# The first half's residual moved from VectorE to ScalarE and an accumulating DMA, in a two-layer convolution kernel on one core

## The chip, the core and the metric

The kernel runs on one core of a Trainium2 chip. The metric is the device time of one execution in microseconds (us). The engines work on queues of their own and meet through semaphores: PE (TensorE, matmuls), DVE (VectorE), ACT (ScalarE), POOL (GpSimd) and SP (SyncE, which here only issues DMAs). Lines such as L847 are lines of the kernel.

## What is computed

The input is 16 images of 128 channels by 64 x 64 pixels. Two layers follow one another, each with a group normalisation (`_gn`) ahead and a residual.

```python
def _L0_conv_ref(x, g_pos, g_neg, bias, input_factor, output_factor):
    v = dac(x * input_factor)
    ...
    patches = unfold2d(v, KH, KW, SH, SW)
    fv = patches + CUBIC * patches ** 3
    g = g_pos - g_neg
    outs = [jnp.einsum('bctfyx,ocyx->btfo', fv, g[i]) for i in range(WP - 1)]
    mem_out = adc(outs[-1])
    for i, bit in enumerate(reversed(range(WP - 1))):
        mem_out = mem_out + adc(outs[i]) * 2.0 ** bit
    mem_out = mem_out * output_factor
    result = mem_out + bias
...
x = x + _L0_conv_ref(_gn(x), ...)
x = x + _L1_conv_ref(_gn(x), Wq, Wk, Wv, B, Wm)
```

The first layer is a 3 x 3 convolution with three sets of weights ("planes"); each plane's sum is rounded and clipped, the three are added with weights, scaled, given a bias and added to x. The second layer projects each pixel to 64-channel queries, keys and values, forms exponential sums, takes a ratio, projects back to 128 channels and adds.

## The kernel before, in words

An image is held in SBUF as one of four buffers `xr`, used in turn, 128 channels by 4096 pixels in f32, and is worked on in four quarters of 1024 pixels (`PX`) or two halves of 2048 (`HPX`). The images run through a software pipeline: in phase p the kernel makes the first layer's convolution of image p, the second layer of image p-1, and the statistics and input rows of image p+1. A phase has 36 slots, `SLOTS = 6 * STEPS`, and each engine has a loop over these slots of its own. Which work stands at which slot is written out by hand in the tables at the head of the file (`X1_STATS`, `BIAS`, `RESIDUAL`, `DOUBLE`, `HIGH`, `Z_ACT` and so on), and within a slot the order of the lines in `phase` decides. A slot number over 35 means a slot of the next phase. An engine works its queue in order, so an instruction that waits holds all that stands behind it.

A phase has six steps n of six slots: two halves h of three planes i. For a step, PE makes six products of the convolution: two into bank B (`low_pair`, at place 0 and 1), two into a bank of A (place 2 and 3), and the last two into that same bank of A one step later (`outer`, place 4 and 5). The banks of A alternate, `A[n % 2]`. At each product two matmuls with the high parts and one with the low parts run for each of three rows of taps (L504 to L506). ScalarE copies bank B to SBUF (`copy_m2`, L839, place 2 of the step), VectorE mixes it with bank A (`mix_middle`, L1195 to L1207), and when the last products are in, ScalarE rounds the bank to int16 (`adc_round`, L847) into the plane's buffer `u[i]`. PE may use a bank of A again when the rounding of two steps earlier is done, which it waits for ahead of its first product into the bank:

```python
if j == 1 and (prev or n >= 2):
    pe.wait_ge(rounded, nth(p, STEPS, n - 2))
```

For step 0 of an image that is the rounding of step 4 of the image before, which stands at slot 0 of ScalarE's queue. Ahead of it, at slot 35, ScalarE doubles plane 0 of the second half (`double`, L855), for which VectorE waits in `combine_planes` (L1213 to L1218, slot 0).

When a half's planes are there, VectorE clips the last, adds it (L1225, L1228) and makes the residual (L1231, slot 23 for the first half, slot 8 of the next phase for the second), `xr = u[1] * fin + xr`. ScalarE has added the bias to `xr` before (`add_bias`, L859, slots 17 and 32). The statistics for the second normalisation are taken by ScalarE from the finished `xr`, two passes for each quarter with accumulation (`channel_stats`, L803 to L812). The quarters of the first half stand at slots 26 and 31, those of the second half at slots 8 and 9 of the next phase, and VectorE reads all four at slot 12.

The second layer of image p-1 runs in quarters: ScalarE makes z (`z_split`, L875 and L880, slots 18, 25, 35, 41), POOL its low part (`z_rest`, L1499), PE the projections (L586, behind the wait for L839), ScalarE the exponentials (L884, L896), VectorE their product with the values (`weighted_values`, L1283), PE the sums (L617), ScalarE the logarithm (L890, L892), VectorE the ratio (L1292 to L1300), PE the projection back (L639), ScalarE the eviction (L904) and POOL an accumulating DMA of 512 KB into `xr` (`add_mix`, L1532). The first layer's input rows are made by ScalarE (L749, L759, L769), VectorE (L1107 to L1151) and POOL (`rows_low`, L1525). SP issues the loads of image p+2 and the stores of finished quarters.

The buffer `shared` holds weights in the making at the start and small pieces afterwards. In the last phases there is no next image, and the second layer of the last two images has slots of its own (`TAIL`).

Of the kernel before, what the change touches and what calls it, by code (L numbers as in the profile page):

```python
# [34 lines left out]
PX = ROWS * W  # L35
# [34 lines left out]
BIAS = (17, 32)  # L70
X1_STATS = (26, 31, 8, 9)
# [31 lines left out]
def conv_layers_kernel(nc, x, g_pos, g_neg, bias, in_factor, out_factor, Wq, Wk, Wv, Bm, Wm, out):  # L103
# [6 lines left out]
    with ctx:  # L110
# [3 lines left out]
        def sem(name):  # L114
            return ctx.enter_context(nc.semaphore(name))
# [10 lines left out]
        shared = sb("shared", [P, NP * 4 * 3 * P + 4 * 3 * P])  # L126
        y2 = [shared[:, k * PX:(k + 1) * PX] for k in range(2)]
# [145 lines left out]
        biased = sem("biased")  # L273
        first_done = sem("first_done")
# [448 lines left out]
        def _(act):  # L723
# [96 lines left out]
            def stats_x1(image, m, q, before):  # L820
                act.wait_ge(first_done, nth(image, HALVES, q // 2))
                channel_stats(1, xr[m], image, q, before)
# [18 lines left out]
            def adc_round(p, n, first):  # L841
                h, i = divmod(n, NP)
                act.wait_ge(conv_ready, nth(p, STEPS, n))
                if not first or h:

                    act.wait_ge(first_done if i else summed, nth(p, HALVES, h - 1))
                nc.scalar.copy(u[i].rearrange("p (t k c) -> p k t c", k=4, c=W)[:, 0:4:3],  # L847
                               A[n % 2][:, :, :].rearrange("p e (t w) -> p e t w", w=W)).then_inc(rounded, 1)
# [8 lines left out]
            def add_bias(p, m, h):  # L857
                xh = xr[m][:, h * HPX:(h + 1) * HPX]
                nc.scalar.activation(xh, xh, ACT.Identity, bias=bcol[:, :]).then_inc(biased, 1)  # L859
# [64 lines left out]
            def phase(p, m, images):  # L924
# [3 lines left out]
                for slot in range(SLOTS):  # L928
# [32 lines left out]
                    if cur and slot in BIAS:  # L961
                        add_bias(p, m, BIAS.index(slot))
# [40 lines left out]
        def _(dve):  # L1003
# [161 lines left out]
            def mix_middle(p, n, images):  # L1165
# [25 lines left out]
                if i == 1 and (prev or h):  # L1191
                    dve.wait_ge(first_done, nth(p, HALVES, h - 1))
# [27 lines left out]
            def first_residual(p, m, h):  # L1220

                xh = xr[m][:, h * HPX:(h + 1) * HPX]
                dve.wait_ge(rounded, nth(p, STEPS, NP * h + 2))
                dve.wait_ge(inner_made, nth(p, STEPS, NP * h + 2))
                nc.vector.tensor_scalar(u[2], u[2], CLIP, -CLIP, ALU.min, ALU.max).then_inc(clipped_last, 1)  # L1225
                dve.wait_ge(summed, nth(p, HALVES, h))
                dve.wait_ge(clipped_last, nth(p, HALVES, h))
                nc.vector.tensor_tensor(u[1], u[1], u[2], ALU.add).then_inc(combined, 1)  # L1228
                dve.wait_ge(combined, nth(p, HALVES, h))
                dve.wait_ge(biased, nth(p, HALVES, h))  # L1230
                nc.vector.scalar_tensor_tensor(out=xh, in0=u[1], scalar=fin[:, :], in1=xh, op0=ALU.mult, op1=ALU.add  # L1231
                                               ).then_inc(first_done, 1)

            def last_residual(m):
# [6 lines left out]
                dve.wait_ge(biased, nth(p, HALVES, h))  # L1241
# [18 lines left out]
            def last_sums(m):  # L1260
# [3 lines left out]
                dve.wait_ge(first_done, HALVES * B)  # L1264
# [84 lines left out]
            def phase(p, m, images):  # L1349
# [3 lines left out]
                for slot in range(SLOTS):  # L1353
# [19 lines left out]
                    if prev and cur and slot == RESIDUAL[1]:  # L1373
                        first_residual(p - 1, before, 1)
# [13 lines left out]
                    if cur and slot == RESIDUAL[0]:  # L1388
                        first_residual(p, m, 0)
# [48 lines left out]
        def _(pool):  # L1438
# [95 lines left out]

            def second_layer(p, m, slot, images):
# [8 lines left out]
            def phase(p, m, images):  # L1544
                prev2, prev, cur, nxt = images
                before, two_before = (m + 3) % RING, (m + 2) % RING
                for slot in range(SLOTS):
                    second_layer(p, m, slot, images)
                    if cur and slot in LOW[2:]:
                        rows_low(p, m % 2, LOW.index(slot))  # L1550
                    if nxt and slot in LOW[:2]:
                        rows_low(p + 1, 1 - m % 2, LOW.index(slot))
# [41 lines left out]
```

## Time and profile before

| | |
|---|---|
| median of 3 runs | 1522.66 us (1522.54 to 1523.33) |
| profiled execution, its own time | 1522.15 us |
| its span, first to last instruction | 1520.4 us |
| mean granted TensorE clock | 0.983 |
| busy: PE, VectorE, ScalarE, POOL | 1430.8, 1400.2, 1193.8, 528.1 us |
| residual L1231 on VectorE | 31 instructions, 85.8 us |
| bias L859 on ScalarE | 32 instructions, 63.9 us |
| accumulating DMAs of 512 KB on POOL | 60 |

The profile shows one execution. Busy time is the time in which an engine had an instruction at work; waits for semaphores and the issuing of DMAs are not in it. A line of the timeline gives the start in us from the span's start, the duration, the engine, the line, the operation, output and input by the program's names, and in brackets the idle time of the engine just before, with what ended it. The granted clock is TensorE's: 1.00 is its upper level of 2.4 GHz and 0.50 its lower level of 1.2 GHz. Consecutive matmuls overlap, so a matmul's duration is longer than the distance between two starts.

### The profile page before, as it was taken

What the parts mean: (1) busy time and instruction counts of PE and PEld (TensorE: products, weight loads), DVE (VectorE), ACT (ScalarE), POOL (GpSimd) and SP (SyncE); (2) the same over time, 40 slices, a digit from 0 to 9 for tenths busy, and PEclk for the clock granted to TensorE, in tenths of its full rate; (3) what the DMA queues carried; (4) which work ended last, traced back from release to release, by engine and by line L of the source; (5) the groups of instructions that cost most, each with busy time, mean ns of one, the idle gap of its engine ahead of it and who ended that gap; (6) DMA issues with size and microseconds to landing.
All of it is one profiled execution on the core that took longest, in us unless ns stands there. A gap on an engine that the chain in (4) does not pass through costs nothing.

```text
span 1520.4 us, 24553 instructions
## 1 busy us (share of the span) xinstructions
PE 1430.8 (94%) x8560; PEld 659.2 (43%) x8560; DVE 1400.2 (92%) x2185; ACT 1193.8 (79%) x1561; POOL 528.1 (35%) x503
## 2 busy tenths in 40 slices
PE   2799999999999999999999999999999999999975
PEld 2444444444444444444444444444444444444432
DVE  6879999999999999999999999999999999999766
ACT  4547788788978878897887889788797978876563
POOL 3111334333433433343343334434333443433312
PEclk9799999999999999999999999999999999999997
DMA  5011011223123222312322231232223123212232
GB/s 209 1 56 42 15 29 46 94 56 111 35 56 105 57 84 56 111 39 56 101 56 84 56 112 37 53 108 56 84 56 112 32 56 108 57 28 57 56 84 84
DMA packets 29181, 103.92 MB, mean 68 GB/s; under 512 B 4032, under 2 KB 4224, under 8 KB 29056
## 3 DMA queue, kind: packets, MB, share of 16 engines
q1 hardware_dynamic: 20416, 70.86, 12.6%
q0 software_dynamic: 8640, 31.46, 10.9%
q8 instruction: 71, 1.16, 0.3%
q14 instruction: 54, 0.44, 0.1%
HBM read 37.29 MB, written 33.55 MB: 47 GB/s over the span
## 4 chain that ended last, share of the span: by engine, by line
DVE 51%; PE 25%; issue 16%; ACT 5%; DVEq 1%; POOL 1%; DMA 0%; SPq 0%; ACTq 0%; POOLq 0%
PE A L504 5%; PE A L506 4%; PE A L505 4%; DVE duo L1135 4%; DVE A L1198 3%; DVE A L1207 3%; DVE uall L1201 3%; DVE uall L1228 3%; DVE duo L1195 3%; DVE uall L1203 3%; DVE A L1199 3%; DVE duo L1196 3%; DVE f L1112 2%; PE B L504 2%; DVE t L1147 2%
## 5 line engine op out<-in xcount | busy, mean ns | idle before, releaser
L504 PE MATMUL A<-T,WH 128*128 128x504 f16 (+1 forms) x1152 | 438.5, 381 | 0.0
L505 PE MATMUL A<-T,WH 128*128 128x504 f16 (+1 forms) x1152 | 437.5, 380 | 0.0
L506 PE MATMUL A<-T,WL 128*128 128x504 f16 (+1 forms) x1152 | 437.5, 380 | 0.0
L1525 POOL TENSOR_TENSOR T<-t,T 128x512 f16<-128x512 f32 x189 | 259.5, 1399 | 421.8 <-ACT T L769 421.8
L1499 POOL TENSOR_TENSOR zl<-z,zh 128x512 f16<-128x512 f32 x120 | 160.5, 1354 | 404.9 <-ACT zh L880 404.9
L812 ACT ACTIVATE junk<-xr,shift 128x1024 f16<-128x1024 f32 x244 | 280.1, 1148 | 5.4
L504 PE MATMUL B<-T,WH 128*128 128x504 f16 (+1 forms) x576 | 222.0, 385 | 19.9 <-DVE T L1161 11.5
L505 PE MATMUL B<-T,WH 128*128 128x504 f16 (+1 forms) x576 | 221.9, 385 | 0.0
L506 PE MATMUL B<-T,WL 128*128 128x504 f16 (+1 forms) x576 | 221.8, 385 | 0.0
L504 PEld LDWEIGHTS A<-T,WH 128*128 128x128 f16 x1152 | 115.4, 100 | 165.5 <-issue 47.6
L506 PEld LDWEIGHTS A<-T,WL 128*128 128x128 f16 x1152 | 112.7, 98 | 136.2
L505 PEld LDWEIGHTS A<-T,WH 128*128 128x128 f16 x1152 | 112.8, 98 | 118.0
L749 ACT ACTIVATE q<-xr,bi,sc 128x1024 int16<-128x1024 f32 x64 | 79.2, 1240 | 68.5 <-DVE f L1112 46.5
L839 ACT COPY m<-B 128x1024 f32<-128x1024 f32 x96 | 95.9, 999 | 36.9 <-PE B L506 36.9
L769 ACT CAST T<-t 128x512 f16<-128x512 f32 x192 | 105.9, 614 | 21.8 <-DVE t L1151 21.7
L847 ACT CAST uall<-A 128x1024 int16<-128x1024 f32 x96 | 96.1, 1002 | 33.3 <-PE A L506 33.1
L504 PEld LDWEIGHTS B<-T,WH 128*128 128x128 f16 x576 | 57.0, 99 | 91.6 <-ACT T L769 11.6
L1532 POOL DMA_DIRECT2D xr<-shared x60 | 53.8, 897 | 108.2 <-ACT shared L904 108.2
L884 ACT ACTIVATE shared<-L 128x512 f32<-128x512 f32 x61 | 36.1, 592 | 70.3 <-PE L L586 70.3
L506 PEld LDWEIGHTS B<-T,WL 128*128 128x128 f16 x576 | 57.1, 99 | 70.2 <-issue 3.6
L505 PEld LDWEIGHTS B<-T,WH 128*128 128x128 f16 x576 | 57.0, 99 | 69.3 <-issue 3.3
L1231 DVE SCALAR_TENSOR_TENSOR xr<-uall,fin,xr 128x2048 f32<-128x2048 int16 x31 | 85.8, 2768 | 1.1
(186 smaller groups left out, 2573.0 us busy)
## 6 DMA issues: line engine op xcount, KB each, us to landing
xr<-in_x_dram SPq DMA_DIRECT2D x64, 512.0 KB, 5.7
out_dram<-xr SPq DMA_DIRECT2D x64, 512.0 KB, 2.7
xr<-shared POOLq DMA_DIRECT2D x60, 512.0 KB, 4.5
xr<-in_L_conv_g_pos_dram SPq DMA_DIRECT2D x3, 576.0 KB, 9.9
xr<-in_L_conv_g_neg_dram SPq DMA_DIRECT2D x3, 576.0 KB, 10.9
xr<-in_L_conv_Wm_dram SPq DMA_DIRECT2D x2, 32.0 KB, 9.0
xr<-in_L_conv_Wq_dram SPq DMA_DIRECT2D x1, 32.0 KB, 11.7
xr<-in_L_conv_Wk_dram SPq DMA_DIRECT2D x1, 32.0 KB, 11.6
```

What stands on the lines that cost most here:

```text
L504: nc.tensor.matmul(to, wh, th, start=fresh and y == 1, stop=False, skip_group_check=True)
L505: nc.tensor.matmul(to, wh, tl, start=False, stop=False, skip_group_check=True)
L506: done = nc.tensor.matmul(to, wl, th, start=False, stop=y == 2, skip_group_check=True)
L749: nc.scalar.activation(q16[b][:, :], xr[m][:, q * PX:(q + 1) * PX], ACT.Identity, bias=bi1[:, :], scale=sc1[:, :]).then_inc(leveled, 1)
L769: nc.scalar.copy(T[:, 0, pair, g * TILES:(g + 1) * TILES, :, :], t32[:, pair]).then_inc(th_ready, 1)
L812: nc.scalar.activation(junk[:, :], src[:, q * PX:(q + 1) * PX], func, bias=shift[which][:, :], accum_out=moments[which][:, k, q:q + 1]).th ...
L839: nc.scalar.copy(m2[:, :, :], low_pair[:, :, :]).then_inc(m2_copied, 1)
L847: nc.scalar.copy(u[i].rearrange("p (t k c) -> p k t c", k=4, c=W)[:, 0:4:3], A[n % 2][:, :, :].rearrange("p e (t w) -> p e t w", w=W)).the ...
L1135: nc.vector.tensor_tensor(flat, f[:, at + 2:at + 2 + ROWS, :], f[:, at:at + ROWS, :], ALU.subtract).then_inc(delta_made, 1)
L1231: nc.vector.scalar_tensor_tensor(out=xh, in0=u[1], scalar=fin[:, :], in1=xh, op0=ALU.mult, op1=ALU.add).then_inc(first_done, 1)
L1499: nc.gpsimd.tensor_tensor(zl[0][:, cols], z32[:, cols], zh[0][:, cols], ALU.subtract).then_inc(zl_ready, 1)
L1525: last = nc.gpsimd.tensor_tensor(low, t32[:, pair, :, :, :].rearrange("p t e w -> p (t e w)"), high, ALU.subtract)
```

## The change

For the first half of each image the bias pass of ScalarE at slot 17 and the residual of VectorE at slot 23 go. VectorE still clips and adds the last plane (now `sum_planes`). ScalarE then writes `y1 = u[1] * fin + bcol` into a free part of `shared` (`first_output`, slot 25), and POOL adds it to `xr` with an accumulating DMA of 1 MB (`first_add`, slot 26). The two statistics passes over the first half wait for that DMA and move from slots 26 and 31 to slots 34 and 35. The waits that protect `u[1]` and `u[2]` are named anew: plane 4's mixing on VectorE waits for `first_output`, and the roundings into `u[1]` and `u[2]` wait for `first_output` and for the sum. The second half is made as before. The change's title also speaks of PE's second layer sorted by shape; the diff has no line of PE.

```diff
-BIAS = (17, 32)
-X1_STATS = (26, 31, 8, 9)
+OUTPUT = 25
+OUTPUT_ADD = 26
+BIAS = 32
+X1_STATS = (34, 35, 8, 9)
...
+        y1 = shared[:, 2 * PX:4 * PX]
...
             def stats_x1(image, m, q, before):
-                act.wait_ge(first_done, nth(image, HALVES, q // 2))
+                if q < 2:
+                    act.wait_ge(first_added, nth(image, 16, 15))
+                else:
+                    act.wait_ge(first_done, nth(image, 1, 0))
...
-                    act.wait_ge(first_done if i else summed, nth(p, HALVES, h - 1))
+                    if i == 0:
+                        act.wait_ge(summed, nth(p, HALVES, h - 1))
+                    elif i == 2:
+                        act.wait_ge(combined, nth(p, HALVES, h - 1))
+                    elif h:
+                        act.wait_ge(y1_made, nth(p, 1, 0))
+                    else:
+                        act.wait_ge(first_done, nth(p, 1, 0, 1))
...
-            def add_bias(p, m, h):
-                xh = xr[m][:, h * HPX:(h + 1) * HPX]
+            def first_output(p):
+
+
+                act.wait_ge(combined, nth(p, HALVES, 0))
+                if isinstance(p, int) and p == 0:
+                    act.wait_ge(small_done, 1)
+                    act.wait_ge(w_turned, 9)
+                else:
+                    act.wait_ge(first_added, nth(p, 16, 15, 1))
+                nc.scalar.activation(y1, u[1], ACT.Identity, bias=bcol[:, :], scale=fin[:, :]).then_inc(y1_made, 1)
+
+            def add_bias(p, m):
+                xh = xr[m][:, HPX:2 * HPX]
                 nc.scalar.activation(xh, xh, ACT.Identity, bias=bcol[:, :]).then_inc(biased, 1)
...
-                if i == 1 and (prev or h):
-                    dve.wait_ge(first_done, nth(p, HALVES, h - 1))
+                if i == 1 and h:
+                    dve.wait_ge(y1_made, nth(p, 1, 0))
+                elif i == 1 and prev:
+                    dve.wait_ge(first_done, nth(p, 1, 0, 1))
...
+            def first_add(p, m):
+
+
+                waits_apart(pool, (y1_made, nth(p, 1, 0)))
+                nc.gpsimd.dma_start(xr[m][:, 0:HPX], y1, accum_op=ALU.add).then_inc(first_added, 16)
```

## Rows read from the trace of the kernel before

**Rows 1.** The page, busy us (share of the span) and number of instructions.

```profile
PE 1430.8 (94%) x8560; PEld 659.2 (43%) x8560; DVE 1400.2 (92%) x2185; ACT 1193.8 (79%) x1561; POOL 528.1 (35%) x503
```

**Rows 2.** Stretches of an image: us, busy us of each engine, PEclk, DMA.

```profile
706.90:795.35 88.45, 86.93 (x528) 39.57 (x527) 85.02 (x133) 74.49 (x99) 33.19 (x31) 1.00 0.26 72
...
sum 707.60, PE 695.89 PEld 317.76 DVE 676.60 ACT 596.35 POOL 263.94; mean PE 86.99 PEld 39.72 DVE 84.58 ACT 74.54 POOL 32.99
```

**Rows 3.** Waits: engine, line, waited for, us in total, times, longest.

```profile
PE L L586 <- ACT m L839: 10.0, 15, 1.1
...
PE L L617 <- DVE shared L1283: 9.1, 15, 0.7
...
ACT q L749 <- POOL bi L1483: 22.0, 16, 2.7
```

**Rows 4.** Timeline of ScalarE, 726 to 755 us.

```profile
726.83 1.00 ACT L839 COPY m<-B 128x1024 f32<-128x1024 f32 x1
...
735.15 1.15 ACT L812 ACTIVATE junk<-xr,shift 128x1024 f16<-128x1024 f32 x1
...
737.57 0.99 ACT L839 COPY m<-B 128x1024 f32<-128x1024 f32 x1
...
740.14 0.60 ACT L884 ACTIVATE shared<-L 128x512 f32<-128x512 f32 x1 [1.58 <-PE L L586]
...
743.73 1.66 ACT L769 CAST T<-t 128x512 f16<-128x512 f32 x3 [0.45 <-DVE t L1151]
...
749.57 1.91 ACT L855 ACTIVATE uall<-uall 128x2048 int16<-128x2048 int16 x1
...
751.38 0.99 ACT L847 CAST uall<-A 128x1024 int16<-128x1024 f32 x1
...
752.27 0.20 ACT L803 ACTIVATE shift<-xr 128x1 f32<-128x1 f32 x1
...
754.93 0.99 ACT L839 COPY m<-B 128x1024 f32<-128x1024 f32 x1
```

**Rows 5.** Timeline of PE, 731 to 754 us.

```profile
731.71 0.38 PE L504 MATMUL B<-T,WH 128*128 128x512 f16 x1
...
738.61 1.05 PE L586 MATMUL L<-zh,wqkv 128*64 128x512 f16 x8 [0.90 <-ACT m L839]
...
744.44 1.09 PE L617 MATMUL L<-shared,eb 64*64 64x256 f32 x16 [0.62 <-DVE shared L1283]
...
753.25 0.38 PE L504 MATMUL A<-T,WH 128*128 128x512 f16 x1
```

**Rows 6.** Timeline of VectorE, 724 to 754 us.

```profile
724.46 2.35 DVE L1231 SCALAR_TENSOR_TENSOR xr<-uall,fin,xr 128x2048 f32<-128x2048 int16 x1
...
734.53 0.68 DVE L1195 TENSOR_TENSOR duo<-A,m 128x512 f32<-128x512 f32 x1
...
753.17 0.68 DVE L1213 TENSOR_SCALAR uall<-uall 128x2048 int16<-128x2048 int16 x1
```

**Rows 7.** PE's timeline at 137.50, and the stretch from 137.34.

```profile
137.50 0.59 PE L504 MATMUL B<-T,WH 128*128 128x512 f16 x1 [2.30 <-issue]
...
137.34:140.75 3.41, 3.25 (x8) 1.17 (x9) 3.34 (x7) 2.66 (x6) 0.06 (x1) 0.50 0.00 0
```

**Rows 8.** The last images: timeline of ScalarE and PE, and the stretch from 1465.13.

```profile
1462.05 1.23 ACT L875 ACTIVATE z<-xr,bi,rs 128x1024 f32<-128x1024 f32 x1
...
1465.09 0.64 PE L586 MATMUL L<-zh,wqkv 128*64 128x512 f16 x2 [2.28 <-DVE shared L1300]
...
1465.13:1468.54 3.41, 3.41 (x18) 1.32 (x18) 0.00 (x0) 2.53 (x3) 2.45 (x3) 0.50 0.14 28
```

**Rows 9.** ScalarE's L875 by shape; L1532's DMAs to landing; POOL's timeline.

```profile
L875 ACT ACTIVATE z<-xr,bi,rs 128x1024 f32<-128x1024 f32 x60 | 73.8, 1230 | 0.0
...
DMA to landing us min/median/max: 4.5/4.5/6.0
...
734.34 3.52 POOL L1525 TENSOR_TENSOR T<-t,T 128x512 f16<-128x512 f32 x3 [5.00 <-ACT T L769]
```

More of the change, by code:

```diff
@@ L273, in conv_layers_kernel @@
         biased = sem("biased")
+        y1_made = sem("y1_made")
+        first_added = sem("first_added")
         first_done = sem("first_done")
@@ L960, in phase @@
                         double(p, DOUBLE.index(slot))
-                    if cur and slot in BIAS:
-                        add_bias(p, m, BIAS.index(slot))
+                    if cur and slot == OUTPUT:
+                        first_output(p)
+                    if cur and slot == BIAS:
+                        add_bias(p, m)
                     if cur and slot in HIGH[2:]:
@@ L1218, in combine_planes, with sum_planes @@
                 nc.vector.tensor_tensor(u[1], u[0], u[1], ALU.add).then_inc(summed, 1)
-            def first_residual(p, m, h):
-                xh = xr[m][:, h * HPX:(h + 1) * HPX]
+            def sum_planes(p, h):
                 dve.wait_ge(rounded, nth(p, STEPS, NP * h + 2))
@@ L1228, in first_residual @@
                 nc.vector.tensor_tensor(u[1], u[1], u[2], ALU.add).then_inc(combined, 1)
-                dve.wait_ge(combined, nth(p, HALVES, h))
-                dve.wait_ge(biased, nth(p, HALVES, h))
+            def first_residual(p, m):
+                xh = xr[m][:, HPX:2 * HPX]
+                dve.wait_ge(combined, nth(p, HALVES, 1))
+                dve.wait_ge(biased, nth(p, 1, 0))
                 nc.vector.scalar_tensor_tensor(out=xh, in0=u[1], scalar=fin[:, :], in1=xh, op0=ALU.mult, op1=ALU.add
@@ L1240, in last_residual @@
                 dve.wait_ge(summed, nth(p, HALVES, h))
-                dve.wait_ge(biased, nth(p, HALVES, h))
+                dve.wait_ge(biased, nth(p, 1, 0))
                 for c in range(2):
@@ L1263, in last_sums @@
                 count = 1.0 * PX
-                dve.wait_ge(first_done, HALVES * B)
+                dve.wait_ge(first_done, B)
                 for h in range(2):
@@ L1373, in phase @@
                     if prev and cur and slot == RESIDUAL[1]:
-                        first_residual(p - 1, before, 1)
+                        sum_planes(p - 1, 1)
+                        first_residual(p - 1, before)
                     if not cur and slot == 3:
@@ L1388, in phase @@
                     if cur and slot == RESIDUAL[0]:
-                        first_residual(p, m, 0)
+                        sum_planes(p, 0)
                     if nxt and slot in QUANTISE:
@@ L1550, in phase @@
                         rows_low(p, m % 2, LOW.index(slot))
+                    if cur and slot == OUTPUT_ADD:
+                        first_add(p, m)
                     if nxt and slot in LOW[:2]:
```

## The prediction

> **What bounds the kernel now.** I read the page's busy line first: PE is busy 94% of the span and VectorE 92%, so either could be the bound [rows 1]. The page's chain runs mostly through VectorE, but a chain cannot tell who has slack, so I went to stretches of one image each: eight of them last 707.60 us, 88.45 us an image, and in the mean PE is busy 86.99 of these, VectorE 84.58, ScalarE 74.54 [rows 2]. The waits of PE settle it. In the steady part it waits at two places only, once an image each: for ScalarE's copy L839 (10.0 us in 15 waits, 0.67 us each) and for VectorE's L1283 (9.1 us in 15, 0.61 us each) [rows 3]. So PE is the bound, and all that the change can gain there is 10.0 + 9.1 = 19.1 us, however much VectorE work it removes.
>
> What PE waits for without showing it has to be read from the order of the work. The first matmuls into bank A of an image (slot 2) wait, at L550, for ScalarE's rounding of plane 4 of the image before (L847 at slot 0). ScalarE ends that rounding at 751.38 + 0.99 = 752.37 [rows 4]; PE starts the matmuls at 753.25 [rows 5]. The slack is 0.88 us. This is the number on which the forecast turns.
>
> **The change, part by part.** The diff touches nothing on PE: the sorting of the second layer in the title has no line in it, and I cost it at nothing.
>
> *VectorE* loses the L1231 of each image's first half, 16 instructions of 2.35 us (one of these at 724.46 [rows 6]). VectorE then comes to plane 4 (734.53) and to L1283 about 2.3 us earlier, which ends PE's wait for L1283. It waits anew for ScalarE's output pass before plane 4: that pass ends near 729.2 (below), and VectorE gets there at 734.53 - 2.35 = 732.2, so the wait costs nothing; if the pass came over 3 us later, VectorE would wait and give back part of the 2.35 us.
>
> *ScalarE, slot 17 to slot 25.* The bias pass of the first half goes. Behind it ScalarE waits for POOL's scale anyway (22.0 us in 16 waits [rows 3]), so no gain. The new pass reads 2048 int16 and writes f32 with a bias and a scale. The nearest rows are L855, of equal width and int16 input (1.91 us at 749.57 [rows 4]), and L875, with both factors, 1.23 us for half the width, so 2.46 us [rows 9]. I take 2.3 us. VectorE's sum is done at 724.46, and ScalarE comes to the pass at 726.83, where the copy of plane 4 (L839) now starts [rows 4, 6]. That copy moves to 729.1 and ends at 730.1; PE needs it at 731.71 [rows 5]. Cover 1.6 us, cost nothing at either bound.
>
> *POOL and the DMA.* One accumulating issue of 1 MB an image is added. POOL waits for the output pass in its queue; the next instruction behind it starts at 734.34 after an idle 5.00 us, so nobody behind it is held [rows 9]. The 512 KB form lands 4.5 us after issue, at most 6.0 [rows 9]. For 1 MB I bound it by 4.5 and 2 x 6.0 = 12 us and take 9: issued near 729.3, landed near 738.3, at the worst 741.3. The statistics that wait for it start near 745 (below). Cost nothing. SP's queue is not touched, and its loads are needed only at slot 0.
>
> *ScalarE, slots 26 and 31 to slots 34 and 35.* Here is the price. Two statistics passes cost 754.93 - 752.27 = 2.66 us (with the shift) and 737.57 - 735.15 = 2.42 us [rows 4], 5.08 us together. At slot 31 the pass stood ahead of the copy L839 for which PE waited; taking it away ends that wait. But it does not leave ScalarE earlier at the end of the image: behind the copy, ScalarE waits for PE (1.58 us before 740.14) and is paced by it [rows 4]. From 740.14 to the rounding at 751.38 ScalarE has one wait, 0.45 us before 743.73; the rest is work back to back, and both statistics now stand inside this stretch, ahead of the doubling and of the rounding.
>
> The sum for this image: ScalarE enters the stretch 0.90 us earlier (PE's wait for the copy, gone), saves the 0.45 us (VectorE's T is earlier), and does 5.08 us more. The rounding ends at 752.37 - 0.90 - 0.45 + 5.08 = 756.10. PE, freed of 0.90 and 0.62 us [rows 5], is ready at 753.25 - 1.52 = 751.73. It stands idle for 4.4 us and goes on at 756.10, 2.85 us later than before. With the mean wait of 0.67 us in place of 0.90 it is 3.08; I take 3.0 us an image. VectorE's gain is not passed on either: its next step waits for the doubling, which ends near 755.1, while it began that step at 753.17 [rows 6].
>
> *What an idle PE costs beyond the wait.* After an idle stretch of 2.30 us PE started at 137.50, and the 3.41 us from 137.34 ran at a granted 0.50, the 1.2 GHz level; near the end, 2.28 us of idle were followed by 3.41 us at 0.50 as well [rows 7, 8]. Work at half speed for 3.41 us costs 1.7 us. The two short waits of an image leave the clock at its full level, 1.00 [rows 2]. The new wait is 4.4 us, longer than either that were followed by the low level, so I add 1.7 us an image. The Trainium skill, "TensorE: Matmul & The Clock Gate" (section on HAM oscillation), warns that waits between bursts of matmuls throw the array back to the low clock and that every round of a loop then pays for it. The trace shows this for single gaps; none of its steady images does. By that rule alone the sum would be the one with the clock term, without it the rival below.
>
> *How often, and the ends.* The two short waits come at 15 places; the full pattern (second layer between slots 21 and 35, next image at slot 2) is there 14 times, from image 1 to image 14. Behind image 0 there is no second layer and ScalarE has waits enough: I count 0. At the tail, z of image 14's last part (1462.05) moves behind one statistics pass, 2.66 us, and PE's start at 1465.09 waits for it [rows 8]; some 2.5 us go to the end.
>
> Sum: 14 x (3.0 + 1.7) + 2.5 = 68.3 us. The profiled execution took 1522.15 us, 0.51 under the median of the three runs, 1522.66. The forecast for the median is 1522.66 + 68.3 = 1591, rounded to **1590 us**. A measurement of this kernel tells about 0.2% (3 us) from no change.
>
> **The rivals.**
>
> *The clock holds.* If the 4.4 us fall so that the low level lies mostly inside the idle stretch, only 14 x 3.0 + 2.5 = 44.5 us are left: **1567 us**. For it: the steady part shows 1.00 throughout; against it: both idle stretches above were shorter. 0.20.
>
> *Faster: PE's two waits go and no new one comes.* Place: the release of bank A at slot 2. Price: the 19.1 us of waits go, **1503 us**. It decides if ScalarE's rounding comes no later than PE's readiness, that is if its stretch from 740.14 takes 4.4 us less than my sum, for instance because the waits that the trace puts on PE there are not what paces ScalarE. For it: VectorE has less to do and all that it feeds comes earlier. Against: the rows of the stretch stand back to back. 0.07.
>
> *Worse than the forecast.* The low clock lasts for two stretches of 3.41 us: 14 x 1.7 = 24 us more, **1614 us**. Or the DMA lands over 16 us after its issue, and each us beyond costs 14 us. For it: 1 MB in one accumulate is nowhere in this trace, and loads of 512 KB run beside it. Against: none of the smaller ones took over 6.0 us. 0.09.
>
> *The parts cancel* (a shorter ScalarE stretch, no low clock): within 3 us of before, **1523 us**. 0.04.
>
> **How the numbers follow.** Forecast 0.60, then 0.20, 0.07, 0.09 and 0.04. Faster holds 0.07, same 0.04, slower 0.60 + 0.20 + 0.09 = 0.89. The range takes in the forecast, the clock rival and the longer low clock, with the per-image term between 2.0 and 3.1 us: 14 x 2.0 + 2.5 = 30.5, so from 1553 to 1614 us.
>
> **What would show it.** Right: in the waits of PE a new entry once an image, bank A waiting for ScalarE's L847 copy, near 4.4 us; the entries for L839 and L1283 gone; the granted clock dips once an image, and PE's share falls below 94%; VectorE's 16 passes gone from its busy time, its idle time larger, ended by the doubling. Wrong: no wait of PE at slot 2, or a wait of ScalarE for the new DMA ahead of the statistics at slot 34, or VectorE waiting for the output pass ahead of plane 4. A steady image under 88.45 us would overturn the whole argument.

## The result, and the profile after

The change makes the kernel slower: 1607.99 us (median of 4 runs, 1606.51 to 1608.83) against 1522.64 us before on the same chip, a ratio of 1.0559 with an interval of 1.054 to 1.0577. That is 85.4 us more where 68.3 were forecast. The sign, the place and the kind of the loss came as predicted; the size was 17 us short.

The page's busy line after, to be read against [rows 1]:

```profile
PE 1459.3 (91%) x8560; PEld 663.8 (41%) x8560; DVE 1391.4 (87%) x2169; ACT 1195.3 (74%) x1561; POOL 555.7 (35%) x519
```

VectorE has 16 instructions less, but only 8.8 us of busy time less, where 16 x 2.35 = 37.6 us were taken away. PE does the same 8560 matmuls and is busy 28.5 us longer, which fits matmuls at a lower clock (below).

The waits after, as engine, line, what it waits for, us in total, times, longest:

```profile
PE A L509 <- ACT uall L862: 57.4, 15, 4.1
...
PE L L622 <- DVE shared L1316: 11.6, 14, 0.9
...
PE L L591 <- ACT m L847: 3.6, 4, 3.1
```

The first row is new. Bank A now waits for ScalarE's rounding (L862, which was L847) in every image: 1.17 us behind image 0, then 4.05 us in 13 images and 3.52 in one. This is the slack of 0.88 us of [rows 4, 5] turned into a wait. The third is what is left of the wait for ScalarE's copy, 10.0 us in [rows 3]: 3.1 of these 3.6 us fall in the last image. But the second, VectorE's L1316 (L1283 before), did not go: it was 9.1 us and is 11.6.

ScalarE's timeline in a middle image, through the stretch that answers to 740 to 755 us of [rows 4] (start, us, engine, line, what, idle before and releaser):

```profile
683.04 2.01 ACT L885 ACTIVATE xr<-xr,bcol 128x2048 f32<-128x2048 f32 x1
685.65 1.66 ACT L774 CAST T<-t 128x512 f16<-128x512 f32 x3 [0.59 <-DVE t L1179]
...
689.50 1.15 ACT L817 ACTIVATE junk<-xr,shift 128x1024 f16<-128x1024 f32 x1
...
694.13 1.14 ACT L817 ACTIVATE junk<-xr,shift 128x1024 f16<-128x1024 f32 x1
...
696.55 1.89 ACT L870 ACTIVATE uall<-uall 128x2048 int16<-128x2048 int16 x1
698.35 0.99 ACT L862 CAST uall<-A 128x1024 int16<-128x1024 f32 x1
```

Each quarter has two passes; the first of each is shown. PE's timeline in the same image:

```profile
686.36 1.09 PE L622 MATMUL L<-shared,eb 64*64 64x256 f32 x16 [0.76 <-DVE shared L1316]
...
699.39 0.61 PE L509 MATMUL A<-T,WH 128*128 128x512 f16 x1 [4.05 <-ACT uall L862]
```

Both statistics stand ahead of the doubling and the rounding, as the diff says, and PE goes on with bank A 0.05 us after the rounding has ended.

These rows and those of before can be cut into two parts, from one such rounding to the next (a middle image in each kernel, not the same one). The rounding of the image before ended at 604.57 + 0.99 = 605.56:

```profile
604.57 0.99 ACT L862 CAST uall<-A 128x1024 int16<-128x1024 f32 x1
```

In the kernel before it ended at 663.61:

```profile
662.62 0.99 ACT L847 CAST uall<-A 128x1024 int16<-128x1024 f32 x1
```

From there to PE's sums (L617 before, L622 after) it was 744.44 - 663.61 = 80.83 us [rows 5], and is 686.36 - 605.56 = 80.80. From the sums to the end of the next rounding it was 752.37 - 744.44 = 7.93 us [rows 4, 5], and is 699.34 - 686.36 = 12.98. So the whole difference between these images, 5.02 us, lies in the second part, and it is the two statistics passes, 5.08 us in [rows 4]. The first part, in which VectorE lost 2.35 us of work, is not a tenth of a us shorter. The other middle images say the same: the second part is 13.0 us in all 13 images with both parts, against 7.9 to 8.2, and the first 80.5 to 81.0 in eight and 81.5 to 82.4 in five, against 80.4 to 80.9 (once 81.7).

Where those 2.35 us went stands in VectorE's and POOL's timelines:

```profile
665.57 1.23 DVE L1257 TENSOR_TENSOR uall<-uall 128x2048 int16<-128x2048 int16 x1
...
669.70 2.18 DVE L1163 TENSOR_TENSOR duo<-f 128x1024 f32<-128x1024 f32 x1
671.80 1.64 DVE L1166 SCALAR_TENSOR_TENSOR duo<-f 128x512 f32<-128x512 f32 x1
...
681.84 1.23 DVE L1163 TENSOR_TENSOR duo<-f 128x1024 f32<-128x1024 f32 x1
```

```profile
669.45 3.45 POOL L1533 TENSOR_TENSOR zl<-z,zh 128x512 f16<-128x512 f32 x2 [6.96 <-ACT zh L906]
```

Beside POOL's subtraction the same two instructions that take 1.23 and 0.69 us at 681.84 and 682.99 in this image took 2.18 and 1.64, together 1.90 us more; and POOL's pair took 3.45 us. In the kernel before, VectorE had reached only its work on PSUM (four instructions from 726.73) when that subtraction ran, and came to the transform behind it. The rows there, POOL's subtraction first, then VectorE's sum, its work on PSUM and the transform:

```profile
727.07 2.27 POOL L1499 TENSOR_TENSOR zl<-z,zh 128x512 f16<-128x512 f32 x2 [7.18 <-ACT zh L880]
```

```profile
723.20 1.22 DVE L1228 TENSOR_TENSOR uall<-uall 128x2048 int16<-128x2048 int16 x1
...
726.73 0.69 DVE L1292 TENSOR_TENSOR L<-L,shared 128x512 f32<-128x512 f32 x1
...
729.71 1.22 DVE L1135 TENSOR_TENSOR duo<-f 128x1024 f32<-128x1024 f32 x1
```

With the residual gone, VectorE is through with the work on PSUM sooner, and the transform slides beside the subtraction. VectorE also starts the sum ahead of all this later: 60.01 us behind the rounding, against 723.20 - 663.61 = 59.59 before. The 0.42 us and the 1.90 us make up the 2.35 but for 0.03.

The clock after, as stretches (us, busy us of PE, PEld, VectorE, ScalarE and POOL, granted clock, DMA share, GB/s):

```profile
605.20:608.61 3.41, 2.99 (x8) 1.05 (x9) 3.17 (x5) 3.26 (x7) 0.00 (x0) 0.50 0.65 148
697.40:704.23 6.83, 4.84 (x12) 1.78 (x13) 5.52 (x8) 6.73 (x11) 0.03 (x1) 0.50 0.59 154
```

Each of the 14 images has one such stretch at 0.50 (1.2 GHz), which begins between 2.0 us ahead of PE's start at bank A and 1.3 us behind it; nine last 3.41 us and five 6.83. From that start of PE to the next one it is 94.5 to 95.4 us behind the five longer ones, and 93.5 to 94.0 behind eight of the shorter (the ninth leads into the last image). Against the same images of before that is 6.5 us more in the mean for the five and 5.0 for the eight, so a longer stretch costs 1.5 us on top, 7.4 us for all five.

At the end there is one wait more, in ScalarE's timeline of the last image and in PE's:

```profile
1515.60 2.09 ACT L881 ACTIVATE shared<-uall,bcol,fin 128x2048 f32<-128x2048 int16 x1 [3.06 <-DVE uall L1257]
1517.60 0.99 ACT L847 COPY m<-B 128x1024 f32<-128x1024 f32 x1
```

```profile
1518.64 1.05 PE L591 MATMUL L<-zh,wqkv 128*64 128x512 f16 x8 [3.08 <-ACT m L847]
```

The output pass waits for VectorE's sum, the copy of bank B stands behind it in ScalarE's queue, and PE waits for the copy.

The two new pieces of work cost what the prediction took for them. ScalarE's output pass takes 2.09 us (2.3 taken), and the DMA answers to [rows 9] so (issues, KB each, median us from issue to landing):

```profile
xr<-shared POOLq DMA_DIRECT2D x60, 512.0 KB, 4.6
xr<-shared POOLq DMA_DIRECT2D x16, 1024.0 KB, 8.1
```

### The profile page after: what moved, and what is told of

Same layout as the page of the kernel before. It is cut to its first block, busy times and chain, and to the rows that moved or that the text cites. A ratio compares the mean times of both kernels' runs of the same rounds, so it can differ in the third digit from the quotient of the medians.

```text
span 1606.5 us, 24563 instructions
## 1 busy us (share of the span) xinstructions
PE 1459.3 (91%) x8560; PEld 663.8 (41%) x8560; DVE 1391.4 (87%) x2169; ACT 1195.3 (74%) x1561; POOL 555.7 (35%) x519
## 4 chain that ended last, share of the span: by engine, by line
DVE 46%; issue 19%; PE 18%; ACT 14%; POOL 1%; DMA 1%; DVEq 1%; SPq 0%; ACTq 0%; POOLq 0%
DVE duo L1163 4%; PE A L509 4%; PE A L510 3%; PE A L511 3%; ACT junk L817 3%; DVE A L1228 3%; DVE duo L1166 3%; DVE A L1237 3%; DVE uall L1231 3%; DVE duo L1225 2%; DVE duo L1226 2%; DVE A L1229 2%; DVE uall L1233 2%; ACT z L901 2%; DVE f L1140 2%
## 5 line engine op out<-in xcount | busy, mean ns | idle before, releaser
L509 PE MATMUL A<-T,WH 128*128 128x504 f16 (+1 forms) x1152 | 450.4, 391 | 57.4 <-ACT uall L862 57.4
L510 PE MATMUL A<-T,WH 128*128 128x504 f16 (+1 forms) x1152 | 448.3, 389 | 0.0
L511 PE MATMUL A<-T,WL 128*128 128x504 f16 (+1 forms) x1152 | 447.3, 388 | 0.0
L1533 POOL TENSOR_TENSOR zl<-z,zh 128x512 f16<-128x512 f32 x120 | 176.5, 1488 | 492.1 <-ACT zh L906 492.1
L509 PEld LDWEIGHTS A<-T,WH 128*128 128x128 f16 x1152 | 117.6, 102 | 235.7 <-ACT uall L862 64.8
L510 PEld LDWEIGHTS A<-T,WH 128*128 128x128 f16 x1152 | 115.1, 100 | 122.3 <-issue 10.7
L847 ACT COPY m<-B 128x1024 f32<-128x1024 f32 x96 | 96.1, 1001 | 60.5 <-PE B L511 32.8
L862 ACT CAST uall<-A 128x1024 int16<-128x1024 f32 x96 | 96.1, 1001 | 43.0 <-PE A L511 43.0
L1163 DVE TENSOR_TENSOR duo<-f 128x1024 f32<-128x1024 f32 x64 | 91.7, 1432 | 7.8 <-POOL T L1559 4.0
L509 PEld LDWEIGHTS B<-T,WH 128*128 128x128 f16 x576 | 56.9, 99 | 91.3 <-ACT T L774 11.6
L1316 DVE SCALAR_TENSOR_TENSOR shared<-L,shared 128x512 f32<-128x512 f32 x61 | 41.8, 686 | 60.4 <-ACT shared L910 59.6
```

The costliest lines, as they stand in the source:

```text
L509: nc.tensor.matmul(to, wh, th, start=fresh and y == 1, stop=False, skip_group_check=True)
L510: nc.tensor.matmul(to, wh, tl, start=False, stop=False, skip_group_check=True)
L511: done = nc.tensor.matmul(to, wl, th, start=False, stop=y == 2, skip_group_check=True)
L847: nc.scalar.copy(m2[:, :, :], low_pair[:, :, :]).then_inc(m2_copied, 1)
L1163: nc.vector.tensor_tensor(flat, f[:, at + 2:at + 2 + ROWS, :], f[:, at:at + ROWS, :], ALU.subtract).then_inc(delta_made, 1)
L1533: nc.gpsimd.tensor_tensor(zl[0][:, cols], z32[:, cols], zh[0][:, cols], ALU.subtract).then_inc(zl_ready, 1)
```

## The experiments

The main theory is that the place of the two statistics passes, ahead of the doubling and the rounding, costs nearly everything, by PE's wait for bank A and by the low clock behind it. The rivals were the new DMA traffic and VectorE's slower instructions.

**The statistics alone.** The kernel before with nothing but the two slots changed:

```diff
-X1_STATS = (26, 31, 8, 9)
+X1_STATS = (34, 35, 8, 9)
```

> The kernel before, with the statistics of the first half moved from slots 26 and 31 to 34 and 35 and nothing else: no new pass, no new DMA, the residual stays on VectorE. Order theory (the two passes stand ahead of ScalarE's rounding of plane 4, for which PE waits before bank A): PE waits 5.08 - 0.88 - 0.67 = 3.5 us an image at bank A and has one dip of the clock worth 1.7 us, 14 times, and 2.5 us at the tail: about 1522.6 + 75 = 1598 us, at least 1575. Traffic theory (the loss comes from the new pass and from the accumulating DMA of 1 MB, which slow the engines beside them): at most 1545 us, and no wait at bank A over 2 us.

It took 1621.49 us, ratio 1.0646 (1.0618 to 1.0674). Its waits:

```profile
PE A L504 <- ACT uall L847: 57.4, 15, 4.1
...
PE L L617 <- DVE shared L1283: 12.8, 14, 0.9
...
PE L L586 <- ACT m L839: 6.2, 15, 0.6
```

The bank's wait is the same to a tenth as with the whole change, without the DMA and with the residual still on VectorE. The two slots alone cost 99 us, 23 us more than the number expected, and more than the change; the rest of the change gives back about 13. Part of that is the clock: in this run 13 of the 14 images have a stretch of 6.83 us at 0.50, against five in the changed kernel. The traffic rival is out, and so is the thought that the move of the residual itself is what hurts.

**Nearly no statistics.** The changed kernel, the first two quarters' passes over 8 columns:

```diff
-nc.scalar.activation(junk[:, :], src[:, q * PX:(q + 1) * PX], func, bias=shift[which][:, :],
+cols = 8 if which and q < 2 else PX
+nc.scalar.activation(junk[:, 0:cols], src[:, q * PX:q * PX + cols], func, bias=shift[which][:, :],
```

> The changed kernel, with the statistics of the first half taken over 8 columns of each quarter in place of 1024 (the rest of the first half's statistics is left out); every instruction, wait and DMA stays. The four passes shrink from 1.15 us to about 0.2 us. Order theory: the wait of PE at bank A goes, the clock stays at 1.00 through the middle images, and what is left is the wait for VectorE's L1316 (0.8 us an image) and the wait in the last image: 1510 to 1527 us. Traffic theory: the pass and the DMA are still there, so the time stays over 1580 us.

It took 1531.48 us, ratio 1.0059 (1.004 to 1.0078), 4 us over the upper end of what was expected. Of PE's waits these are left:

```profile
PE L L622 <- DVE shared L1317: 11.7, 14, 0.9
...
PE A L509 <- ACT uall L863: 9.6, 14, 1.0
```

None of the 14 images has a stretch at 0.50 any more. 76 of the 85 us hang on the length of these passes. The wait at L622 is still there, so it does not come from the statistics, and without them nothing is gained over the kernel before, though VectorE has a pass less to do.

**One quarter nearly free**, to see whether the wait goes with the length of the work:

```diff
-cols = 8 if which and q < 2 else PX
+cols = 8 if which and q == 1 else PX
```

> The changed kernel, with the statistics of the second quarter alone (slot 35) taken over 8 columns in place of 1024; the rest of that quarter's statistics is left out. Order theory: ScalarE's stretch is 2 x 0.85 = 1.7 us shorter, so PE's wait at bank A falls from 4.2 to about 2.5 us an image, 14 x 1.7 = 24 us. The clock tells the rest: idle stretches of 2.3 us were followed by 0.50 in the kernel before, so I expect the dips to stay in most images, 1584 us; if the clock needs longer idle stretches than this one, the dips go and it is 24 us less, 1560 us. Rival (the time goes with the number of passes on ScalarE, not with where PE waits): 14 x 1.7 us at most and the wait at bank A unchanged.

It took 1576.92 us, ratio 1.037 (1.0353 to 1.0388), between the two numbers expected. The wait at bank A is 33.6 us in 14 images, 2.4 each, halfway between 0.7 with hardly any passes and 4.05 with both: it goes with the length of the work ahead of the rounding. The low clock was still there in 12 of the 14 images, for 3.41 us each.

**VectorE's work put back.** The changed kernel with a pass of 1536 columns on VectorE where the residual stood (its result is overwritten before use):

```diff
+dve.wait_ge(combined, nth(p, HALVES, 0))
+dve.wait_ge(mid_mixed, nth(p, STEPS, 3))
+nc.vector.scalar_tensor_tensor(out=duo_flat, in0=u[1][:, 0:PX + HALF], scalar=fin[:, :],
+                               in1=duo_flat, op0=ALU.mult, op1=ALU.add).then_inc(idle_made, 1)
+dve.wait_ge(idle_made, nth(p, 1, 0))
```

> The changed kernel, with a pass of the same kind as the removed residual put back on VectorE at slot 23 (1536 wide where the residual was 2048 wide, about 1.9 us, into scratch that is written anew before it is read). Order theory: VectorE waits 3.3 us an image for the doubling, so the work is hidden: 1600 to 1620 us. If VectorE's freed time had been worth its length, 16 x 1.9 = 30 us come on top: about 1638 us.

It took 1617.94 us, ratio 1.0629 (1.0609 to 1.0649): 10 us more than the change, 0.6 us for each of the 16 passes, which take 1.82 us each. Some of it is again the clock: eight images have the stretch of 6.83 us, against five. VectorE's groups by shape, in this kernel:

```profile
L1164 DVE TENSOR_TENSOR duo<-f 128x1024 f32<-128x1024 f32 x64 | 78.1, 1220 | 5.8 <-POOL T L1565 1.8
...
L1167 DVE SCALAR_TENSOR_TENSOR duo<-f 128x512 f32<-128x512 f32 x64 | 43.7, 683 | 0.0
```

and in the changed kernel:

```profile
L1163 DVE TENSOR_TENSOR duo<-f 128x1024 f32<-128x1024 f32 x64 | 91.7, 1432 | 7.8 <-POOL T L1559 4.0
...
L1166 DVE SCALAR_TENSOR_TENSOR duo<-f 128x512 f32<-128x512 f32 x64 | 57.2, 893 | 0.0
```

With work in that place the two instructions are back at their old durations; without it they take 13.6 + 13.5 = 27.1 us more over the run, of the 37.6 us that the change took off VectorE.

**The last image's output pass later**, behind the copy for which PE waits:

```diff
-if cur and slot == OUTPUT:
+if cur and slot == (OUTPUT if nxt else 27):
...
-if cur and slot == OUTPUT_ADD:
+if cur and slot == (OUTPUT_ADD if nxt else 27):
```

> The changed kernel, with the output pass and its DMA of the last image alone at slot 27, behind ScalarE's copy for plane 4 and the exponential of slot 26. If the wait of PE at 1518.64 in the last image (3.5 us between two matmuls, and 3.41 us at the low clock behind it) comes from the output pass standing ahead of that copy, it goes: 3.2 + 1.7 = 4.9 us less, about 1603 us. If it comes from something else in the tail: 1608 us as before.

It took 1602.93 us, ratio 1.0528 (1.0505 to 1.0551): 5 us less, as expected. The wait of 3.1 us is gone from PE's waits, and with it the stretch at 0.50 behind it; the next one, some 30 us later, lasts 6.83 us in place of 3.41.

**The bias pass away from the stretch.** In the changed kernel L885 stands at 683.04, ahead of the cast for T:

```diff
-BIAS = 32
+BIAS = 17
```

> The changed kernel, with the second half's bias pass (2.0 us) at slot 17 in place of 32, so out of ScalarE's stretch ahead of the rounding. If ScalarE's stretch alone paces bank A, the wait falls from 4.2 to 2.2 us: 14 x 2.0 = 28 us, about 1580 us or 20 us less where dips of the clock go with it. If VectorE's T at slot 29, which ScalarE waits for 0.6 us ahead of L774 even now, paces the stretch, ScalarE waits 2.0 us longer there and nothing is gained: 1600 to 1610 us.

It took 1609.15 us, ratio 1.0575 (1.0559 to 1.0592): nothing gained by taking 2.0 us out of ScalarE's stretch. Its ScalarE shows why:

```profile
685.42 1.66 ACT L774 CAST T<-t 128x512 f16<-128x512 f32 x3 [2.50 <-DVE t L1179]
```

The idle time ahead of the cast grew from 0.59 to 2.50 us. So the stretch that counts begins with T from VectorE, and not, as the prediction had it, with the start of ScalarE's row of work at 740.14.

**The transform earlier**, to get it out of the way of POOL's subtraction:

```diff
-TRANSFORM = (26, 29, 3, 11)
+TRANSFORM = (23, 29, 3, 11)
```

> The changed kernel, with VectorE's first input transform (L1163 to L1179) at slot 23 in place of 26, so ahead of the ratio of slot 24 and no longer beside POOL's L1533. Collision theory (VectorE's freed 2.35 us were eaten because L1163 and L1166 ran beside L1533 and took 2.18 and 1.64 us in place of 1.22 and 0.68): they take 1.22 and 0.68 again, L1533 gets shorter too, and T of slot 29 comes 1.9 us earlier. ScalarE gains only the 0.6 us that it waits for T, so PE goes on at bank A 0.6 us earlier an image: 14 x 0.6 = 8 us, about 1600 us, while the wait for L1316 falls from 0.9 to under 0.3 us and the wait at bank A grows by about 0.5. If the durations are of another cause, they stay and the time stays at 1608 us.

It took 1609.3 us, ratio 1.0568 (1.0552 to 1.0584): no gain, where 1600 was expected. The collision was not avoided but moved to the next two instructions, in VectorE's timeline:

```profile
668.20 1.38 DVE L1178 TENSOR_TENSOR t<-duo 128x256 f32<-128x256 f32 x1
669.50 1.37 DVE L1179 TENSOR_TENSOR t<-duo 128x256 f32<-128x256 f32 x1
```

They take 0.42 us each elsewhere, so the price is 1.9 us again.

**The statistics of the kernel before, slot 31 to 29**, to see whether PE's two waits there were a gain to be had:

```diff
-X1_STATS = (26, 31, 8, 9)
+X1_STATS = (26, 29, 8, 9)
```

> The kernel before, with the second quarter's statistics at slot 29 instead of 31 and nothing else. At 31 they stand directly ahead of the copy L839 for which PE waits 0.67 us an image; at 29 they use up to 1.1 us of waits of ScalarE that stand ahead of slots 30 and 31. Order theory: that wait goes, 14 x 0.67 = 9 us, about 1513 us. Against it: the rounding of slot 30 and the high rows come up to 1.9 us later, and VectorE's T at slot 29 with them; if these are then late, it is 1520 to 1530 us.

It took 1521.81 us, ratio 1.0006 (0.9994 to 1.0017): no difference. Its waits:

```profile
PE L L617 <- DVE shared L1283: 13.0, 15, 0.9
...
PE L L586 <- ACT m L839: 6.2, 15, 0.8
```

3.8 us went from the wait for the copy, and 3.9 us came to the wait behind it. The two waits of [rows 3] are not 19.1 us of separate gains; PE arrives earlier at the second by what it saves at the first.

**The doubling on VectorE.** The doubling leaves ScalarE's stretch; VectorE clips at half the bounds and doubles in its sum:

```diff
-if cur and slot in DOUBLE:
-    double(p, DOUBLE.index(slot))
...
-dve.wait_ge(doubled, nth(p, HALVES, h))
-nc.vector.tensor_scalar(u[0], u[0], 2.0 * CLIP, -2.0 * CLIP, ALU.min, ALU.max).then_inc(clipped, 1)
+dve.wait_ge(rounded, nth(p, STEPS, NP * h))
+dve.wait_ge(inner_made, nth(p, STEPS, NP * h))
+nc.vector.tensor_scalar(u[0], u[0], CLIP, -CLIP, ALU.min, ALU.max).then_inc(clipped, 1)
...
-nc.vector.tensor_tensor(u[1], u[0], u[1], ALU.add).then_inc(summed, 1)
+nc.vector.scalar_tensor_tensor(out=u[1], in0=u[0], scalar=2.0, in1=u[1], op0=ALU.mult, op1=ALU.add
+                               ).then_inc(summed, 1)
```

> The changed kernel, with ScalarE's doubling pass removed (1.9 us twice an image, one of them in the stretch ahead of the rounding) and the factor 2 folded into VectorE's sum, which becomes a scalar_tensor_tensor instead of a tensor_tensor (1.2 to 2.1 us, so up to 0.9 us more, twice an image). Order theory: the wait at bank A falls by 1.9 us to about 2.3; VectorE no longer waits for the doubling, but its dense stretch ahead of slot 33 gets 0.9 us longer. With dips of the clock as before about 1594 us, without them about 1570. Rival (VectorE's work is what counts): 14 x 1.8 us more, about 1633 us.

It took 1583.18 us, ratio 1.0399 (1.038 to 1.0417), between the two numbers expected. The wait at bank A fell to 32.8 us; on PE's timeline of two neighbouring images:

```profile
684.65 0.60 PE L509 MATMUL A<-T,WH 128*128 128x512 f16 x1 [2.25 <-ACT uall L862]
...
778.13 0.39 PE L509 MATMUL A<-T,WH 128*128 128x512 f16 x1 [2.25 <-ACT uall L862]
```

This run priced the clock, since such a wait was followed by the low level in six images (in one of these it was 3.29 us, in all others 2.25) and not in the other eight. The stretches behind these two waits, and two whole images from rounding to rounding, the first with the low level in it:

```profile
684.70:688.11 3.41, 3.41 (x9) 1.21 (x10) 3.38 (x3) 3.35 (x6) 0.70 (x1) 0.50 0.71 135
778.20:781.61 3.41, 3.41 (x17) 1.51 (x18) 3.38 (x3) 3.37 (x6) 0.68 (x1) 1.00 0.70 135
...
606.52:699.89 93.37, 89.29 (x529) 40.41 (x528) 87.31 (x133) 71.50 (x98) 36.56 (x32) 0.98 0.30 80
699.89:791.69 91.80, 87.68 (x530) 39.77 (x529) 86.72 (x131) 71.16 (x98) 37.13 (x32) 1.00 0.30 81
```

In 3.41 us PE starts 9 matmuls in place of 17, and the image is 1.57 us longer.

**And the first quarter ahead of T.** To that, the output pass and its DMA in two quarters, so that the first quarter's statistics can stand at slot 31:

```diff
-X1_STATS = (34, 35, 8, 9)
+X1_STATS = (31, 35, 8, 9)
...
-nc.gpsimd.dma_start(xr[m][:, 0:HPX], y1, accum_op=ALU.add).then_inc(first_added, 16)
+for c in range(2):
+    waits_apart(pool, (y1_made, nth(p, 2, c)))
+    cols = slice(c * PX, (c + 1) * PX)
+    nc.gpsimd.dma_start(xr[m][:, cols], y1[:, cols], accum_op=ALU.add).then_inc(first_added[c], 16)
```

> The run before this one, and besides the output pass and its DMA in two quarters, so that the first quarter's statistics can stand at slot 31 again; the second quarter's stay at 35. Order theory: another 2.66 us leave the stretch ahead of the rounding, the wait at bank A is under 0.5 us, no dips of the clock in the middle images, and PE may wait up to 0.7 us more for the copy of slot 32: 1525 to 1550 us. Rival (the accumulating DMA and the pass themselves cost the time): two DMAs and two passes an image cost more, not less, over 1590 us.

It took 1548.12 us, ratio 1.0185 (1.0163 to 1.0208). The wait at bank A is gone (1.3 us, once, is left), and another stands at the head of PE's waits, for ScalarE's copy:

```profile
PE L L591 <- ACT m L847: 31.7, 17, 3.4
```

That is up to 3.4 us, where 0.7 was expected at most, and two middle images still have a stretch at 0.50, where none was expected.

**All the mends together**: the doubling on VectorE, the bias at slot 17, the transform at slot 23, the first quarter's statistics at slot 32, the last output pass later (the DMA in one piece again):

```diff
-BIAS = 32
-X1_STATS = (34, 35, 8, 9)
+BIAS = 17
+X1_STATS = (32, 35, 8, 9)
...
-TRANSFORM = (26, 29, 3, 11)
+TRANSFORM = (23, 29, 3, 11)
```

> The changed kernel with five edits: doubling folded into VectorE's sum, the bias pass at slot 17, the first transform at slot 23, the first quarter's statistics at slot 32 (where the DMA has landed, 8.1 us after its issue), and the last image's output pass at slot 27. Order theory with T as the second pacer: from the copy of the queries on, ScalarE has 2.66 + 1.56 + 0.92 + 1.15 + 2.2 + 2.42 + 0.99 = 11.9 us up to the end of the rounding, against 11.05 us on PE up to bank A: a wait of 0.85 us an image, no dips, no wait for L1316, no wait of the last image. That is some 0.4 to 0.7 us an image under the kernel before: 1510 to 1520 us. If the collision or the accumulating DMA costs more than I count, over 1530 us.

It took 1531.15 us, ratio 1.0064 (1.005 to 1.0077): 77 us better than the change, and still 9 us over the kernel before, and over the 1510 to 1520 expected. Of the wait for bank A 0.6 us, once, is left, and no low clock in the middle images; an image takes 89.3 us. PE waits for VectorE:

```profile
PE L L622 <- DVE shared L1316: 13.0, 15, 0.9
```

and VectorE has the collision in two instructions, as at slot 23 above:

```profile
641.42 1.38 DVE L1176 TENSOR_TENSOR t<-duo 128x256 f32<-128x256 f32 x1
642.73 1.38 DVE L1177 TENSOR_TENSOR t<-duo 128x256 f32<-128x256 f32 x1
```

**The subtraction moved, not the transform.** To that, ScalarE's output pass ahead of z in slot 25, so that POOL's subtraction comes about 2 us later, beside VectorE's work on PSUM:

```diff
+if cur and nxt and slot == OUTPUT:
+    first_output(p)
 second_layer(p, m, slot, images)
...
-if cur and slot == (OUTPUT if nxt else 27):
+if cur and not nxt and slot == 27:
     first_output(p)
```

> e11 with one step moved: ScalarE makes the output pass of the first half ahead of its pass for z in slot 25, not behind it, so that GpSimd's subtraction for zl starts 2.1 us later, where VectorE works with the operands from PSUM (its L1325 group) and no longer on the transform. In e11 the image takes 89.3 us against 88.5 before, no PE wait for bank A is left, VectorE is busy almost without a break, and two of its additions took 1.38 in place of 0.42 us beside that subtraction. Theory (VectorE's work in its order sets the image now, and the collision is 1.92 us of it): the additions are back at 0.42, the image at 87.5 to 88.6, 1508 to 1522 us. Rival (the image is paced elsewhere, at PE's wait for the key gate at L622 through other work): the additions fall back but the time stays within 3 us of 1531. Second rival: zl comes too late for PE, a new wait of PE at L591 for zl, over 1535.

It took 1524.06 us (11 runs) against 1522.39 (15 runs), ratio 1.0012 (1.0001 to 1.0022); the time lies 2 us over the range of the theory, and most middle images, at 88.6 to 89.1 us, at its upper end or a little over. VectorE's two instructions are back:

```profile
639.58 0.42 DVE L1178 TENSOR_TENSOR t<-duo 128x256 f32<-128x256 f32 x1
639.91 0.42 DVE L1179 TENSOR_TENSOR t<-duo 128x256 f32<-128x256 f32 x1
```

The wait at L622 is gone (0.3 us, once, is left), and the one for bank A is back, at 0.7 us:

```profile
PE A L509 <- ACT uall L862: 9.2, 13, 1.5
```

So moving one pass on ScalarE that takes as long as before gave 7 us for 14 images. That the end of the collision did it is what the rows show, but the same move also shifts z and what follows from it, which was not tried apart. The collision is not wholly gone either: VectorE's next pass with operands in SBUF, L1135 on `q` at 642.91, started beside the end of the subtraction and took 0.94 us in place of 0.41. The run also shows that the next bound stands right behind. No version tried here beats the kernel before.

## Why the prediction was right in kind and 17 us short

*The main step held.* The statistics stand ahead of the rounding, PE waits for it at bank A, 4.4 us forecast and 4.1 measured. The statistics alone gave the same wait to a tenth, and it went with the length of the passes. The stretch from PE's sums to the rounding grew by 5.05 us, the two passes' 5.08. That ScalarE's stretch begins at 740.14 did not hold: the run with the bias at slot 17 shows that it begins with T.

*The clock held.* 1.7 us an image were forecast; every one of the 14 images has a stretch at 0.50, and the run with the doubling on VectorE priced 3.41 us of it at 1.57. That five images show 6.83 us is a part of the rival "worse than the forecast" that came true. So the rule that the prediction drew from the Trainium skill, "TensorE: Matmul & The Clock Gate" (section on HAM oscillation), agrees with this trace. The ground that the prediction gave, a wait longer than two that were followed by the low level, is weaker than it looks: the last section has a longer one that was not.

*The copies and the DMA cost nothing, as forecast,* in the steady images: the wait for L839's copy went, and the statistics never waited for the DMA of 8.1 us (9 taken).

*The step that failed* is "VectorE then comes to plane 4 (734.53) and to L1283 about 2.3 us earlier, which ends PE's wait for L1283". VectorE did not come there earlier: the part of the image from the rounding to the sums took 80.80 us, as 80.83 before. Of the 2.35 us, 1.90 went into the two instructions beside POOL's subtraction, and 0.42 into VectorE's later start of the sum. PE's low clock at the image's start is the likely reason for the latter: in the five images with the longer low stretch that sum starts later still, 60.7 to 61.6 us behind the rounding, against 59.7 to 60.2 in the eight others. PE's wait there grew by 2.5 us where 9.1 were forecast to go, which is 11.6 us of the sum.

*Why the wait at bank A came out near 4.4 all the same.* The prediction let ScalarE enter the stretch 0.90 us earlier and saved 0.45 us of its wait for T, and on PE's side it took off 0.90 and 0.62. All four stand or fall with T, by which ScalarE's cast and PE's sums start alike. When T came no earlier, both sides stayed where they were: the wait hardly changes by that, the image's length does.

*The tail was mis-sized.* "Some 2.5 us go to the end", for z behind a statistics pass, was near (PE's idle time there went from 2.28 to 4.43 us). What it left out is the output pass ahead of the copy in the last image, where VectorE's sum comes late: 3.1 us of wait and the low clock behind it, 5 us by the run that moved it.

*The 17 us.* The wait at L1316 makes 11.6, the tail 2.15 + 5 - 2.5 = 4.7, and bank A's wait takes off 14 x 4.4 - 57.4 = 4.2. That is 12.1. The five longer stretches at 0.50 make 7.4 more, and 3.41 us at 0.50, priced at 1.57 us in place of 1.7, takes off 14 x 0.13 = 1.8. That comes to 17.7, against the 17.1 missing; the parts come from single traces and hold to a us or two. What made five of the stretches longer stays open.

*The rivals.* "The clock holds" fell by the rows at 0.50. "Faster" fell, and the run at slot 29 shows that its 19.1 us were never there: one wait passes on to the next. "The parts cancel" fell as well.

## What to carry to other kernels

When work is moved from a busy engine to one with spare time, look at where in the queue it lands: 5 us of passes, behind which PE had waited 0.67 us, cost over 5 us an image once they stood between the last input of a stretch and the rounding that frees a bank. Two waits of an engine in one loop are not two gains: ask what the later one is paced by before adding them up. And work taken off an engine changes what runs beside what, so look at which instructions slide together, not only at how much is left.

## What the runs showed of the hardware that was not expected

VectorE and POOL slowed each other where both had f32 operands in SBUF: VectorE's addition of 128 x 1024 took 2.18 us in place of 1.23, the scalar_tensor_tensor of 128 x 512 1.64 in place of 0.69, the addition of 128 x 256 1.38 in place of 0.42, and POOL's pair of subtractions 3.45 us beside the longer two and 2.67 beside the shorter, in place of 2.27. The rise is 0.95 or 0.96 us for each of these VectorE instructions, whatever its length, and each pair of subtractions shown caught two. A pass with a single input, L1135 in the last run, rose less, from 0.41 to 0.94 us; it started 0.66 us before the subtraction ended. VectorE's work with operands in PSUM ran beside the same subtraction in the last run without such a rise (0.69 to 0.70 us). The Trainium skill, "SBUF — State Buffer" (section on who interferes with whom), says that a VectorE instruction with two inputs in SBUF contends with a GpSimd instruction that reads SBUF, and that the shared pair of ports behind this is an exclusive lock. The trace agrees: an addition that does not grow with the length is what waiting for a POOL instruction to end would leave.

The same wait of 2.25 us at the same place was followed by 3.41 us at 0.50 in one image and by the full clock in the next. Nor does the longer idle stretch decide by itself: in the kernel before with the statistics at slot 29, PE stood idle for 3.12 us at the place where [rows 7] has 2.30, and went on at the full clock.

```profile
138.14 0.38 PE L504 MATMUL B<-T,WH 128*128 128x512 f16 x1 [3.12 <-issue]
...
138.10:141.50 3.40, 3.36 (x16) 1.59 (x17) 3.33 (x6) 2.54 (x5) 0.00 (x0) 1.00 0.00 0
```

What decides between the two was not tried.
